# Moving keys, values and the memory summary into a quantised feed-forward layer

## The reference

```
x += tanh(ga[0]) * causal_attention(ln(x), ctx, ctx)           # 16 heads of 16
x += tanh(gf[0]) * quantised_ffn(ln(x))                        # 256 -> 2*704 -> 256
x += tanh(ga[1]) * memory(ln(x), ctx)
x += tanh(gf[1]) * (ln(x) @ sum_r(factors[r]) / sqrt(8) + bias)  # "mixing"
x += tanh(ga[2]) * softmax(ln(x) @ ctx.T / 16, mask) @ ctx     # "third attention"
x += tanh(gf[2]) * mixture_of_8_experts(ln(x))
x += tanh(ga[3]) * attention(ln(x), keys, values)              # keys and values from ctx
x += tanh(gf[3]) * mixture_of_7_experts(ln(x))
```

```
# quantised_ffn: q(v) = clip(round(v / s), -127, 127) * s, s = max|v| of a row / 127
gate, up = split(q(xn) @ q(w_gate_up).T)       # 704 each
out = q(silu(gate) * up) @ q(w_down).T
# memory: one summary row per sequence
s_t = sigmoid(decay) * s_(t-1) + ctx_t @ W_in.T + b_in
summary = mean_t(s_t @ W_out.T + b_out)
y = ln(x) + summary;  out = (y - mean(y)) / sqrt(var(y) + eps) * gamma + beta
# last attention: K = rms_norm(ctx @ w_k_img.T + b), V = ctx @ w_v_img.T + b
```

## Time and profile before

| | |
|---|---|
| median of three runs | 992.5 us (991.85 to 997.67) |
| the profiled execution | 992.77 us |
| its span, first to last instruction | 990.9 us |
| busy: PE / DVE / ACT / POOL | 816.9 / 641.0 / 430.3 / 324.7 us |
| mean granted TensorE clock | 0.848 of 2.4 GHz |

### The profile page before, as it was taken

How to read it: one execution, slowest core, us unless ns; L and a number is a source line. 1 busy time by engine, 2 the same in 40 slices (tenths; PEclk the granted TensorE clock), 3 DMA queues, 4 the chain that set the end, 5 groups by cost and what they waited for, 6 DMA issues and landing times. The chain is left out here.

```text
span 990.9 us, 17287 instructions
## 1 busy us (share of the span) xinstructions
PE 816.9 (82%) x4572; PEld 515.2 (52%) x4572; DVE 641.0 (65%) x1515; ACT 430.3 (43%) x932; POOL 324.7 (33%) x582
## 2 busy tenths in 40 slices
PE   0699997676756879898898997999998889999990
PEld 0445554233322335566766884856665745666650
DVE  8488996689884766655922226378886676544445
ACT  0456674345551452222224773857666213333320
POOL 2000004233325452202683774410002286134340
PEclk9789999755556999655599998989999589999995
DMA  9300007999304008903253544510001322223217
GB/s 328 94 21 20 21 11 226 309 288 344 98 0 131 1 0 302 273 0 143 86 177 101 155 139 120 163 23 20 19 12 30 121 86 82 63 74 94 88 42 254
DMA packets 90275, 112.96 MB, mean 114 GB/s; under 512 B 11685, under 2 KB 81864, under 8 KB 89050
## 3 DMA queue, kind: packets, MB, share of 16 engines
q1 hardware_dynamic: 83434, 95.20, 32.3%
q0 software_dynamic: 6768, 16.86, 4.8%
HBM read 51.10 MB, written 58.42 MB: 111 GB/s over the span
## 5 line engine op out<-in xcount | busy, mean ns | idle before, releaser
L756 ACT ACTIVATE probs_t<-ps 128x1024 f32<-128x1024 f32 x64 | 65.5, 1023 | 71.2 <-PE ps L1651 71.2
L608 POOL COPY work<-ctx_rows 128x256 f32 (+1 forms) x32 | 12.6, 397 | 213.1 <-PE ps L1662 213.1
L1122 DVE TENSOR_REDUCE row_max<-ps 128x8 f32<-128x1024 f32 x64 | 78.0, 1219 | 5.6 <-PE ps L1641 2.9
L1128 DVE TENSOR_TENSOR work<-ps,row_max 128x1024 f32<-128x1024 f32 x64 | 77.7, 1214 | 3.4
L1493 DVE TENSOR_TENSOR ctx_cols<-ps,ctx_rows 128x512 f32<-128x512 f32 x54 | 37.3, 691 | 59.3 <-PE ps L2062 59.1
L988 ACT ACTIVATE ctx_cols<-ctx_cols 128x256 f32<-128x256 f32 x54 | 22.5, 417 | 117.1 <-DVE ctx_cols L1493 117.1
L1651 PE MATMUL ps<-ident,work 128*128 128x128 f32 x512 | 69.9, 280 | 2.3 <-ACT work L750 2.1
L2062 PE MATMUL ps<-early,xt 128*128 x152 | 71.5, 593 | 0.0
L1651 PEld LDWEIGHTS ps<-ident,work 128*128 128x128 f32 x512 | 56.7, 142 | 17.3 <-ACT work L750 12.4
L585 POOL DMA_INDIRECT y_rows<-ctx_cols,w2d x38 | 37.6, 990 | 81.1 <-DMA y_rows<-ctx_cols,w2d 44.9
L2082 PE MATMUL ps<-early,ctx_cols 128*128 (+1 forms) x216 | 55.9, 381 | 4.3 <-ACT ctx_cols L993 4.3
(11 more groups left out here) (333 smaller groups left out, 2001.4 us busy)
## 6 DMA issues: line engine op xcount, KB each, us to landing
x_rows<-pad_row SPq DMA_DIRECT2D x1, 17415.0 KB, 68.3
work<-x_rows SPq DMA_DIRECT2D x77, 129.0 KB, 2.1
x_rows<-pad_row SPq DMA_DIRECT2D x1, 7740.0 KB, 34.4
x_rows<-pad_row SPq DMA_DIRECT2D x1, 7611.0 KB, 39.5
early<-in_w3st SPq DMA_DIRECT2D x8, 512.0 KB, 4.1
work<-y_rows SPq DMA_DIRECT2D x16, 256.0 KB, 3.0
early<-y_rows SPq DMA_DIRECT2D x8, 512.0 KB, 7.7
late<-in_w2u SPq DMA_DIRECT2D x1, 2304.0 KB, 47.1
```

Of the source, the lines that this page charges most:

```text
L756: act.activation(probs_t[:, :, :], ps[:, 4:6, :], ACT.Copy).then_inc(sem("att.evac"), 1)
L1122: dve.tensor_reduce(row_max[:, u, 8 * c:8 * c + 8], scores(c), AX.X, ALU.max).then_inc(sem("att.max"), 1)
L1128: dve.tensor_tensor(probs[:, u, c, :].rearrange("p (h k) -> p h k", k=P), scores(c), row_max[:, u, 8 * c:8 * c + 8].unsqueeze(2).to_broadc ...
```

## The change

Three things, and what follows from them:

1. **Keys, values and the summary go into the quantised layer.** Per tile PE does, in this order: turn and gate-up of the next tile, one step of the summary (tiles 0 to 3 only), the six turns of h, the turn of the keys of two tiles before, keys and values of this tile (bank 7), down. ACT takes the rounding of x from DVE, and squares, scales and copies keys between its passes. Both bf16 passes (DVE line 1207, ACT line 819) are gone: PE turns the rounded f32 numbers, which still hold the rounding constant, and ACT takes it off in the copy out of PSUM, which writes bf16. Gate and up stand side by side in banks 0 to 2 (`gu_cols`). The first x scale stands inside the first attention's last steps, the first gate-up ahead of the selector matmuls. The loops of this stage are written out on PE, ACT, DVE and POOL.
2. **The memory layer is alone**, and its `y` is taken as x * rstd + summary in one DVE operation instead of xn + summary (the mean that is left out is taken off by the layer norm of y). `norm_x(2, ...)` is gone. POOL takes `deviation(1)` and `deviation(2)` pair by pair between other work.
3. **No wait for the whole mixing at the start of the third attention:** PE waits for `resid3` only ahead of the first product that writes bank 4, and DVE norms the third attention's first pair ahead of the mixing's last statistics.

w3kv is loaded at the start, into `late`; `kt_all` and `v_all`, the finished keys and values, stand in `early`, and so `fac` moves. SP's queue: the first half of the x_rows3 pads goes ahead of w2u, w2u after the last keys and values, and the stores of keys and values ahead of w3up.

The core of the diff (SP, ACT and PE; DVE and POOL keep their operations but for what is said above):

```diff
@@ SP
             pad(x_rows2, 0, NB2)
+            pad(x_rows3, 0, NB3 // 2)
             sp.wait_ge(sem("mem.s3"), 1)
+            sp.wait_ge(sem("kv.mm"), NT)
...
             sp.dma_start(w2u, a["w2u"]).then_inc(sem("load.w2"), 16)
...
-            pad(x_rows3, 0, NB3 // 2)
@@ POOL
+            def key_rms(t, u):
+                pool.wait_ge(sem("kv.sq"), t + 1)
+                pool.tensor_scalar(rms_e[:, u, 1:2], ss[:, u, 1:2], 1.0 / D, RMS_EPS, ALU.mult, ALU.add
+                                   ).then_inc(sem("kv.mean"), 1)
+                pool.wait_ge(sem("kv.mean"), t + 1)
...
+                TT(rms[:, u, 1:2], rms_e[:, u, 1:2], consts[:, 0:1], ALU.pow).then_inc(sem("kv.rms"), 1)
...
                 for u in range(2):
+                    if not (first and u == 0):
+                        key_rms(t + u - 1, 1 - u)
                     if not last:
                         layernorm1(t + u + 2, u)
...
+                if t + 4 < NT:
+                    dev1(t + 4, False, False)
@@ ACT
+            for t in range(NT):
+                u = t % 2
+                act.wait_ge(sem("qf.g"), t + 1)
+                act.activation(gact[:, u], gact[:, u], ACT.Silu).then_inc(sem("qf.silu"), 1)
+                if t + 1 < NT:
+                    x_round(t + 1, 1 - u)
+                if t:
+                    key_square(t - 1, 1 - u)
+                if t + 1 < NT:
+                    x_evac(t + 1, 1 - u)
...
+                act.wait_ge(sem("qf.hrs"), t + 1)
+                act.activation(gact[:, u], gact[:, u], ACT.Identity, scale=hsc[:, u, 2:3],
+                               bias=consts[:, 3:4]).then_inc(sem("qf.hround"), 1)
+                if t:
+                    key_scale(t - 1, 1 - u)
...
+                act.wait_ge(sem("qf.htr"), t + 1)
...
+                act.activation(hqt[:, 0:5], ht_cols[:, 0:640].rearrange("p (k n) -> p k n", k=5), ACT.Identity, bias=consts[:, 4:5])
+                act.activation(hqt[0:64, 5], ht_cols[0:64, 640:768], ACT.Identity, bias=consts[0:64, 4:5]).then_inc(sem("qf.hout"), 1)
+                if t >= 2:
+                    key_out(t - 2)
@@ DVE
+                    dve.scalar_tensor_tensor(yb[:, u], x[:, t + u, :], rstd[:, bass.ds(t + u, 1)], bank(u, D), ALU.mult, ALU.add
+                                             ).then_inc(sem("xn"), 1)
...
+                if last:
+                    norm_x(4, 0)
                 tile_stats(4, t, sem("resid3"))
@@ PE
+            x_turn(0, 0)
+            gate_up(0, 0)
+            pe.wait_ge(sem("dec.sel"), 1)
+            for b in range(NT):
+                op = mm(ps[0:NT, 3, 0:D], wsel[:, b, :], ctx_rows[:, b, :], start=(b == 0), stop=(b == NT - 1))
+            op.then_inc(sem("mem.c"), 1)
...
+            for t in range(NT):
+                u = t % 2
+                if t + 1 < NT:
+                    wait(pe, sem("kv.out"), t - 2)
+                    x_turn(t + 1, 1 - u)
+                    gate_up(t + 1, 1 - u)
+                if t < 4:
+                    memory_step(t)
+                pe.wait_ge(sem("qf.hround"), t + 1)
+                wait(pe, sem("qf.hout"), t)
+                for k in range(6):
+                    w = min(P, I0 - k * P)
+                    op = pe.transpose(ht_cols[0:w, k * P:(k + 1) * P], gact[:, u, k * P:k * P + w], ident[:, :])
+                op.then_inc(sem("qf.htr"), 1)
+                if t >= 2:
+                    turn_keys(t - 2)
+                keys_values(t)
+                pe.wait_ge(sem("qf.hout"), t + 1)
+                wait(pe, sem("qf.y"), t)
...
```

More of the change, by code:

```diff
@@ L392, in _ @@
             sp.dma_start(mask_u8, a["mask"]).then_inc(sem("load.mask"), 16)
+            for dst, name in ((w3kv, "w3kv"), (qk_c[:, 0:6], "qk_c")):
+                sp.dma_start(dst, a[name]).then_inc(sem("load.w3kv"), 16)
             sp.wait_ge(sem("bias.part"), 5)
@@ L1255, in _ @@
-            dve.wait_ge(sem("mem.s"), 5)
-            dve.tensor_copy(summ3[0:NT, 2], summ[:, 1]).then_inc(sem("mem.s3"), 1)
-            def ffn0(t0, first, last):
-                for u in range(2):
-                    t = t0 + u
-                    if not (last and u):
-                        x_round(t + 1, 1 - u)
-                    scale_gu(t, u)
-                    h_scale(t, u)
-                    if not (first and u == 0):
-                        ffn0_out(t - 1, 1 - u)
-                    if u == 1 and not first:
-                        tile_stats(2, t0 - 2, sem("resid1"))
@@ L1761, in gate_up, with memory_step @@
                 op.then_inc(sem("qf.gu"), 1)
+            def memory_step(t):
+                wait(pe, sem("kv.scaled"), t)
+                if t in (0, 2):
+                    k = t // 2
+                    pe.wait_ge(sem("mem.c_out") if k == 0 else sem("mem.m_out"), 1)
+                    for j in range(2):
+                        op = pe.transpose(ps[:, 7, j * NT:(j + 1) * NT], summ[:, k, j * P:(j + 1) * P], ident[0:NT, 0:NT])
+                    op.then_inc(sem("mem.t"), 1)
+                else:
+                    k = t // 2
+                    pe.wait_ge(sem("mem.t_out"), k + 1)
+                    for j in range(2):
+                        op = mm(ps[0:NT, 7, 0:D], summ_t[:, k, j, :], (w_in, w_out)[k][:, j, :], start=(j == 0), stop=(j == 1))
+                    op.then_inc(sem("mem.m"), 1)
@@ new lines, in keys_values @@
+            def keys_values(t):
+                if t in (0, 2):
+                    pe.wait_ge(sem("mem.t_out"), t // 2 + 1)
+                elif t == 1:
+                    pe.wait_ge(sem("mem.m_out"), 1)
+                elif t == 3:
+                    pe.wait_ge(sem("mem.s"), 1)
+                wait(pe, sem("kv.scaled"), t)
+                mm(bank(7), ones3[32:35, :], b_kv, start=True, stop=False)
+                for j in range(2):
+                    op = mm(bank(7), ctx_cols[:, t, j, :], w3kv[:, j, :], start=False, stop=(j == 1))
+                op.then_inc(sem("kv.mm"), 1)
```

375 lines of the change are left out of this document (163 added, 212 removed).

## The result

The changed kernel takes 966.7 us (median of 4 runs, 963.1 to 968.3) against 992.2 beside it: ratio 0.973, 95% interval 0.968 to 0.978. 967 was forecast. Its profiled execution took 966.25 us, its span 964.4 against 990.9, so 26.5 us went.

| point | before | after | change | forecast |
|---|---|---|---|---|
| first attention's last row transposes | 165.67 | 163.98 | -1.7 | |
| first h scale | 187.67 | 172.74 | -14.9 | |
| last h scale | 295.61 | 281.59 | -14.0 | -10.7 |
| first memory pair | 305.19 | 292.82 | -12.4 | -10.7 |
| second memory pair | 319.05 | 299.44 | -19.6 | -17.9 |

A forecast was written before the change was run, and what follows sets the result against it. The prediction took the quantised layer as DVE bound, at 14.69 us a pair. Its terms, -10.7 - 7.2 - 5.3 - 3.5 + 2 + 0.5 - 1.5 = -25.7, took 992.77 to 967 us; range 954 to 982.

The forecast's parts named there:

- A pair at 13.5: Quantised layer: two tiles take 13.5 us against 14.7, 6.5 even to odd by ACT's queue, 7.0 odd to even by DVE.
- The high level in the layer: Quantised layer: TensorE is granted 2.4 GHz, not 1.2; rival that it stays at 1.2: 1022 us, chance 0.06.
- The start: Layer's start: first gate-up no longer waits for the summary, 167.2 instead of 181.36; with the pairs, last h scale -10.7 us.
- From last h scale to memory at 9.4, 0 us: Last h scale to first memory pair: 9.4 us now and 9.4 after, so 0 us.
- First memory pair -7.2: Memory layer: the first pair's 13.86 us becomes a normal pair and some 0.4, 6.7 us: -7.2.
- Memory pairs at 6.3 because the norm goes: Memory layer: norm_x(2) goes, so a pair takes 6.3 us against 7.18, six times: -5.3.
- To the mixing -3.5: Last memory pair to mixing: 8.55 us becomes 5.9, -2.6; key transposes no longer ahead of the first mixing ones, -0.9.
- Mixing +2: Mixing's start: TensorE idles before it and starts at the low level, two pairs more at 1.0 us each: +2 (0 to 5).
- Code +0.5: Unrolled code has to be fetched while pad writes hold the DMA engines: +0.5 us, with +14 kept for the range.
- the rival with late code: Code arrives late behind the pads, one whole 14.4 us wait: 981 us, chance 0.09.
- Border -1.5: Mixing to third attention: norm_x(4, 0) goes ahead of the statistics, first norm at 402.9 instead of 404.38: -1.5 us.
- The rule on transposes: Quantised layer: full clock does not engage for transposes, so only the tile's products could help it to 2.4 GHz.

The follow-up runs named there:

- half product: Changed kernel with only the first of the two 128-row halves of the keys' and values' product: ratio 0.973, span 963.5.
- late key copies: Changed kernel with ACT's two key copies of a tile behind the next SiLU instead of ahead of it: ratio 0.973, span 965.0.
- repeat: The changed kernel measured once more, without an edit: 966.3 us, ratio 0.975, span 963.3.
- reordered end: Changed kernel with TensorE's and POOL's work at the layer's end reordered; a second run also put key_rms and the mixing's scale behind beta(0): ratios 0.973 and 0.971.
- combination: Changed kernel with reordered tail, late statistics copy, eight unused TensorE products ahead of the mixing, and the summary's small DVE operations at the layer's end: 957.2 us, ratio 0.964.
- late pads: Changed kernel with the pad writes behind the loads of w2u and w3q instead of ahead of the quantised layer: ratio 0.975, span 964.8.

## Why the prediction was right

The total was right and the mechanism in the main as well: the layer rose to the high level, its pair fell to about 13 us, the first memory pair became like the others. That the total hit within 1 us is in part luck. The layer and the border gave more than forecast, the way from the layer to the memory layer, the memory pairs and the mixing gave less, and these errors cancelled. 1.7 of the 26.5 us between the two spans stand ahead of the change.

- **A pair at 13.5.** It is 12.94. Even to odd was forecast at 6.5 by ACT's queue and is 6.44; the half product leaves it at 6.43, so it is not TensorE; the late key copies take 0.14 off, and then DVE waits 1.09 us for POOL's norm. So POOL's queue, costed at nothing here with up to 0.9 us if ACT turned out faster, is next, by that much. Odd to even was forecast at 7.0 by DVE and is 6.50: the stretch of before from which I took 4.7 us held a statistics copy of 0.41 under an add of POOL, and it now takes 0.22; that is 0.2 of the 0.5, and the rest has no run of its own.
- **The high level in the layer** held, but for tile 4: there TensorE idles 2.6 us behind the summary's chain, and in the first trace and the repeat the level falls to 0.66 in 205 to 215. Tiles 5, 6 and 8 were slow (7.79, 7.01, 7.19); in the last two a statistics copy was held (0.72 and 0.54), which explains a part of it. So tile 4 to 15 took 73.7 us where 74.0 were forecast, for other reasons.
- **The start.** Tile 4 came at 207.92, not 211.1. This is nearly all of the layer's surplus of 3.3 us: gate-up started at 165.5 rather than 167.2, tile 1's h scale came at 182.4 rather than 184.3, and the next three steps (7.7, 7.0, 10.8) each fell 0.3 to 0.6 short of the forecast 8.0, 7.4 and 11.4. The first 1.7 us of this are the head start that the trace had ahead of the change; net of it the layer gave 12.3 where 10.7 were forecast.
- **From last h scale to memory at 9.4, 0 us.** It is 11.2 (11.1 counted from the h scale's end, as the sum was). The sum had keys and values at 2.2; they took 3.5 at the low level, and the first summaries stood behind key turns. The reordered end changes both, and POOL's order with them, and gives 3.6 us in all; no run separates the shares, but half of the product alone gives 1.5 us.
- **First memory pair -7.2.** Right (13.86 to 6.62).
- **Memory pairs at 6.3 because the norm goes.** 6.50, so from the second pair to the last 4.5 us went and not 5.3. The reason given holds for a third of it: the norm is 0.23 a pair, and 0.45 have to do with POOL's adds lying on DVE's norms before.
- **To the mixing -3.5.** Right: 5.84 against 5.9 for the last stretch.
- **Mixing +2.** From its first norm to the third attention's first, with the border's 1.6 added back, it is 37.5 us in the first trace and 34.8 in the repeat, against 33.7: +3.8 and +1.1. Some 1.3 of either is not the level: the last five steps from norm to norm take 20.1 us even in the combination, where every product takes 1.13, and 18.7 before. Four of them are a steady pair of 3.95 instead of 3.75 us with the same instructions on DVE, in all thirteen traces of the changed kernel and its variants. The pair's gaps are "issue" of 0.66 instead of 0.56 and 0.12 more ahead of the aggregate; it is there with pad writes beside it (late pads) and without, and its cause stays open. What is left for the level is 2.5 us in the first trace and nothing in the repeat: the +2 is a matter of chance.
- **Code +0.5.** Zero in the layer, by the late pads. So the rival with late code is out there.
- **Border -1.5.** 1.6 at the norm, and 2.1 more that I had not seen, from a first pair that now runs at the high level. This is also why the third attention is 2.5 us shorter than before (27.2 against 24.7 in the table), although the prediction called a changed length behind 404 a sign of being wrong.
- **The rule on transposes** (the Trainium skill's page "TensorE: Matmul & The Clock Gate", "Part 4: PE-mode transpose"). In the steady layer ten f32 transposes a tile (two of x, six of h, two of the keys) stand among products, and the grant is 1.00. So the rule did not decide here: no stretch of the layer held transposes alone.

## What to carry to other kernels

Cut a wait at the head of a long chain first, since the chain keeps most of it (4.0 of 5.2 us here), and look at its tail, where an engine has no next tile and its order of work suddenly matters. When several queues are within 0.1 us of each other, an operation that is moved for one of them lands on another: read what it runs beside, not only what it waits for. And before a term is credited to an operation that goes, ask which of its microseconds were its own and which its neighbour's. Before two traces are compared behind an edit, compare them ahead of it: here they differed by up to 2.4 us before the edited code had begun.

## What the runs showed of the hardware

**DVE's copy is held by GpSimd.** A DVE `COPY` of four f32 numbers a row took 0.16 to 0.17 us with GpSimd idle (0.21 once in some 700). In the fourteen traces 82 such copies began under a GpSimd operation on 256 columns or more. All of them ended either at their usual time or 0.02 to 0.04 us after that operation, whichever was later; 73 were held in this way, for up to 0.74 us. Under GpSimd's operations on one or two columns, 112 times, a copy took at most 0.23. One that was held:

```profile
217.40 0.73 POOL L652 TENSOR_TENSOR x<-x,o_n 128x256 f32<-128x256 f32 x1
217.44 0.72 DVE L1035 COPY mv<-mv 128x4 f32<-128x4 f32 x1
218.07 0.41 DVE L1221 TENSOR_REDUCE amax<-xn 128x1 f32<-128x256 f32 x1
218.09 0.73 POOL L670 TENSOR_TENSOR wgb<-wgb,early 128x256 f32<-128x256 f32 x1
218.78 0.93 DVE L1231 SCALAR_TENSOR_TENSOR work<-ps,amax,mid 128x704 f32<-128x704 f32 x1
```

The reduction behind it ran its usual 0.41 beside the next add. The Trainium skill's page "SBUF — State Buffer", section "SBUF: two separate sides", says that DVE and GpSimd share a port pair under an exclusive lock that one holds for its whole instruction, and that on DVE's side it concerns two-port modes and operations with two SBUF inputs. These traces agree: the copy waits, the reduction with one input doesn't.

**The granted level is not set by the program alone.** The first gate-up, the same instructions behind the same work, took 2.53 us in one trace of the changed kernel and ran at 1.00 in the next; the stretch 350 to 360 in the mixing had 0.69 and 1.00. The six runs of the combination spread by 8.1 us, the four of the half product by 0.4.
